# Local attention on one Trainium2 core: the fifth projection of a tile placed ahead of the second group's scores on TensorE

## What is computed

```python
def attn_layer(x, Wqkv, qs, ksc, Wo):          # x (8, 256, 128); 16 heads of 64
    q, k, v = jnp.split(x @ Wqkv, 3, -1)       # 3 x 1024 columns
    q, k = l2norm(q) * qs, l2norm(k) * ksc     # per head
    q = q * cos * scale + rotate_half(q) * sin * scale
    k = k * cos * inv + rotate_half(k) * sin * inv
    out = local_attention(q, k, v)             # windows of 32, each sees itself and the one before
    return out @ Wo

def ffn_layer(x, g, bln, W1, b1, W2, b2):
    a, gate = jnp.split((layernorm(x) * g + bln) @ W1 + b1, 2, -1)
    return a * gelu(gate) @ W2 + b2

for i in range(6):
    x = attn_layer(shift_tokens(x), ...) + x
    x = ffn_layer(shift_tokens(x), ...) + x
```

## Time and profile before

| what | value |
|---|---|
| median of 3 runs | 2246.68 us (2245.82 to 2247.02) |
| the profiled execution | 2248.77 us, its span 2247.0 us |
| TensorE matmul busy | 2105.5 us, 94% |
| TensorE weight load busy | 1439.5 us, 64% |
| VectorE busy | 1842.6 us, 82% |
| ScalarE busy | 1660.0 us, 74% |
| GpSimd busy | 1654.5 us, 74% |
| mean granted TensorE clock | 0.979 |

### The profile page before, as it was taken

How to read it: one execution, slowest core, us unless ns; L and a number is a source line. 1 busy time by engine, 2 the same in 40 slices (tenths; PEclk the granted TensorE clock), 3 DMA queues, 4 the chain that set the end, 5 groups by cost and what they waited for, 6 DMA issues and landing times. The chain is left out here.

```text
span 2247.0 us, 70768 instructions
## 1 busy us (share of the span) xinstructions
PE 2105.5 (94%) x26387; PEld 1439.5 (64%) x26387; DVE 1842.6 (82%) x2689; ACT 1660.0 (74%) x3300; POOL 1654.5 (74%) x1553
## 2 busy tenths in 40 slices
PE   5899869999889999999999999999999999999995
PEld 3555436666646676667676676667667666676764
DVE  4898967777778888888888888888888888888883
ACT  5898845454368788788878878887887887888773
POOL 4677852333378888888888888888888888888881
PEclk8999999999999999999999999999999999999996
DMA  2222220000012223232322322232232222223221
GB/s 77 104 69 67 64 77 1 2 1 1 8 47 77 70 61 79 71 81 61 81 70 59 81 70 76 67 79 72 59 81 70 71 72 74 78 58 82 70 66 45
DMA packets 103501, 140.43 MB, mean 62 GB/s; under 512 B 63376, under 2 KB 64400, under 8 KB 103056
## 3 DMA queue, kind: packets, MB, share of 16 engines
q1 hardware_dynamic: 103440, 139.64, 23.0%
HBM read 56.39 MB, written 1.31 MB: 26 GB/s over the span
## 5 line engine op out<-in xcount | busy, mean ns | idle before, releaser
L1740 PE MATMUL f_psA<-f_W,f_xT 128*128 (+1 forms) x1154 | 603.4, 619 | 7.7 <-ACT f_Vt L1492 3.6
L1630 DVE TENSOR_TENSOR f_m<-f_psA,f_tab 128x1024 f32<-128x1024 f32 x385 | 460.0, 1215 | 78.5 <-ACT f_sq L1474 78.5
L1410 POOL TENSOR_TENSOR f_qkr<-f_qkr,f_rn 128x1024 f32<-128x1024 f32 x192 | 361.4, 1904 | 17.2 <-POOL f_rn L1433 17.2
L1381 POOL TENSOR_TENSOR f_Pr<-f_Pr,f_rden 128x384 f32<-128x384 f32 x384 | 308.1, 835 | 87.2 <-DVE f_rden L1619 87.2
L1474 ACT ACTIVATE f_sq<-f_psA 128x512 f32<-128x512 f32 x385 | 222.2, 590 | 107.0 <-PE f_psA L1740 103.5
L1740 PEld LDWEIGHTS f_psA<-f_W,f_xT 128*128 128x128 f32 x1154 | 192.6, 190 | 131.2 <-issue 90.5
L1606 DVE TENSOR_REDUCE f_mx<-f_psS 128x8 f32<-128x768 f32 x192 | 183.9, 958 | 83.6 <-PE f_psS L1775 83.6
L1400 POOL TENSOR_TENSOR f_qkr<-f_m 128x512 f32<-128x512 f32 x192 | 244.7, 1274 | 7.5 <-DVE f_m L1630 7.5
L1401 POOL TENSOR_TENSOR f_qkr<-f_m 128x512 f32<-128x512 f32 x192 | 246.4, 1283 | 0.0
L795 POOL TENSOR_TENSOR x_Es<-x_E 128x512 f32<-128x512 f32 x64 | 81.4, 1272 | 188.8 <-PE x_psO L1012 127.7
L1661 DVE TENSOR_REDUCE f_ssq<-f_sq 128x32 f32<-128x2048 f32 x96 | 218.5, 2276 | 0.0
(11 more groups left out here) (176 smaller groups left out, 4710.8 us busy)
## 6 DMA issues: line engine op xcount, KB each, us to landing
f_V<-f_Vt SPq DMA_DIRECT2D x96, 384.0 KB, 4.5
f_V<-f_Vt SPq DMA_DIRECT2D x96, 256.0 KB, 3.7
f_W<-in_f_W SPq DMA_DIRECT2D x48, 344.0 KB, 4.6
m_Cb<-m_BC_rows SPq DMA_DIRECT2D x64, 256.0 KB, 3.2
f_W<-in_f_W SPq DMA_DIRECT2D x48, 296.5 KB, 4.2
f_V<-f_Vt SPq DMA_DIRECT2D x48, 128.0 KB, 2.3
f_xsA<-xall SPq DMA_DIRECT2D x98, 32.0 KB
f_xsA<-xall SPq DMA_DIRECT2D x98, 31.8 KB
```

What stands on the lines that cost most here:

```text
L1381: pool.tensor_tensor(pv, pv, rv.unsqueeze(3).broadcast_to([P, 2, 2, KEYS]), ALU.mult).then_inc(Pr_ready[g][j], 1)
L1410: pool.tensor_tensor(qv, qv, rv.unsqueeze(3).broadcast_to([P, 2, GH, DH]), ALU.mult).then_inc(qkr_ready[g], 1)
L1630: dve.tensor_tensor(m12[:, j, :, half].rearrange("p m (h d) -> p m h d", d=DH), psA[n % 2][:, :].rearrange("p (h d) -> p h d", d=DH).unsqu ...
L1740: pe.matmul(psA[n % 2][:, :], xT[:, t, :], weights(i, W_QKV + n * 512, 512), start=True, stop=True).then_inc(A_full[n_fill], 1)
```

## The change

Projection 4 moves from point 8 of the list to a place between points 5 and 6: behind `times_v(1)` and ahead of `scores(1)`. Its wait on `A_free[2]` goes with it. Nothing else is added, removed or moved; the other engines' programs are the same.

```diff
@@ -1882,6 +1882,9 @@
                 if "C" in stages:
                     times_v(0)
                     times_v(1)
+                if "A" in stages:
+                    pe.wait_ge(A_free[2], u + 1)
+                    project(u, i, t, 4)
                 if "B" in stages:
                     scores(1)
                 if "E" in stages:
@@ -1895,9 +1898,6 @@
                     for tt in range(TPB):
                         ins = pe.transpose(psD[0][:, tt * P:(tt + 1) * P], hatC[:, tt, :], ident[:, :])
                     ins.then_inc(xn_full, 1)
-                if "A" in stages:
-                    pe.wait_ge(A_free[2], u + 1)
-                    project(u, i, t, 4)
                 if "C" in stages:
 
                     weights_here(pe, i - 1, share_of(W_2))
```

## The result

The changed kernel takes 2267.38 us (median of 4 runs, 2266.81 to 2268.53) against 2246.25 us for the kernel before in the same session: a ratio of 1.0096, 95% interval 1.0079 to 1.0114. It is slower by 21 us; forecast were 18. The profiled execution has a span of 2266.7 us, 19.7 more than before, at the same mean clock of 0.979.

What follows compares the result with a forecast made beforehand. It took a loop through TensorE for most of a slot, and VectorE at `scores(1)`, to set the pace. D slot + 0.52 and E slot - 0.12 us, times 46 pairs, added 18.4 us: 2265.1 us, range 2248 to 2282.

Steps and rivals of the forecast that it cites:

- The delay of `scores(1)`: On TensorE, the second group's scores start 0.74 us later, behind a 0.17 us step and a 1.05 us projection.
- TensorE's own balance: On TensorE, 0.74 us lost at the scores, 0.86 won back behind: output projection and next slot 0.12 us earlier.
- End of the D slot: Through ScalarE, 0.22 us of the delay is absorbed; the Gelu and first square hold TensorE to + 0.52 us.
- End of the E slot: Through VectorE, the residual sum and the square of projection 0 come out level at the table product: -0.12 us.
- Sum: Whole loop: + 0.52 - 0.12 = + 0.40 us per pair, 46 pairs, + 18.4 us, median 2265.1 us.
- a plain tie: On TensorE at `w1(0, 2)`: it had just arrived there, at 1414.37, the product's start, when the Gelu ended.
- hardly anything else holds TensorE up for long: On TensorE, the 0.27 us wait ahead of `scores(1)`, 89 times, was read as nearly the only long one.
- the faster case: TensorE saves 0.42 us per slot and the delay, 0.44 us, is absorbed: 2237 us; chance 0.13.
- The cheap case: On TensorE, the projection costs 0.86 us in its new place too, delay 0.55 us: + 1 us, 2248; chance 0.10.
- That VectorE passes its delay too: In the E slot, VectorE is 0.19 us late at the table product: + 0.71 per pair, 2279 us; chance 0.12.
- The change between tiled and whole-array work: On TensorE, switching costs 0.15 to 0.23 us going in and 0.19 us in the projection.

Runs made afterwards that it cites:

- e1: The kernel before with the whole projection 4 ahead of the second group's scores in D slots only: 2271.39 us, ratio 1.0111.
- e3: The changed kernel with the second group's exponentials taken over 4 of 8 heads in D slots: 2253.17 us.
- e5: The changed kernel with the third Gelu behind the squares and its product behind the transposes of q and k: 2250.65 us, ratio to before 1.0014.
- e4: The kernel before with the second group's exponentials taken over 4 of 8 heads in D slots: 2238.15 us, ratio 0.9958.
- e6: The kernel before with the third Gelu behind the squares and its product behind the transposes of q and k: 2235.78 us, ratio 0.9952.
- e10: The kernel before with the first half of projection 4 early in both kinds of slot, the Gelu where it was: 2244.36 us, ratio 0.9987.
- e8: The kernel before with projection 4 early, whole in E slots and its first half in D slots, and the third Gelu behind the squares: 2228.52 us, ratio 0.9920.
- e9: The kernel before with the first half of projection 4 early in both kinds of slot and the third Gelu behind the squares: 2226.91 us, ratio 0.9909.

## Why the prediction was right

The forecast was 2265.1 us and + 18.4; measured 2267.4 and + 21. The sum was built per pair (33.25 us predicted, 33.26 measured), so each term can be laid beside the trace.

- *The delay of `scores(1)`*: 0.74 predicted, 0.72 measured. The projection's 1.05 us in its new place was 1.06, the step ahead of it 0.15 us and not 0.17. The price came from projection 1, which stood in the same surroundings; with the 0.86 us of the old place the forecast's own sum gives 2248.
- *TensorE's own balance*: 0.12 us won predicted, 0.15 measured at the start of the output projection. In the D slot the output projection then takes 0.05 us longer (1420.75 - 1418.91 = 1.84 us against 1.78), which the forecast did not have; it costs nothing here, because the Gelu holds TensorE anyway.
- *End of the D slot*: + 0.52 predicted. From the start of `times_v(1)` to projection 2 of the next slot it is 1425.19 - 1415.60 = 9.59 us against 1416.06 - 1406.98 = 9.08: + 0.51. e1 shows it alone (+ 0.52 us per pair, + 24.8 us), e3 and e5 show that it runs through ScalarE: shorten the chain by 0.32 us and 0.33 us per pair come back; take the Gelu out of the way of the squares, 0.37 us, and 0.36 us come back, where the same two edits give 0.19 and 0.23 us in the kernel before.
- *End of the E slot*: - 0.12 predicted. 1442.59 - 1432.30 = 10.29 us against 1433.55 - 1423.17 = 10.38: - 0.09. TensorE reaches the transposes of q and k 1441.30 - 1432.30 = 9.00 us behind `times_v(1)` and before 1432.31 - 1423.17 = 9.14, so it is 0.14 us early; 0.05 of this is lost to VectorE, with which the forecast had the squares level. The rows of these starts that were not shown yet, projection 2 of the changed kernel

```profile
1442.59 1.12 PE L1740 MATMUL f_psA<-f_W,f_xT 128*128 x2
```

and, before,

```profile
1423.17 1.10 PE L1815 MATMUL f_psP<-f_PT,f_V 96*64 96x64 f32 x32
```

- *Sum*: + 0.42 per pair, times 46 is 19.3 us, and the spans differ by 19.7. (Between D slots' `scores(1)` a pair is + 0.41.)

What was off lies in the reading of the kernel before. The text held that TensorE arrived at the E slot's gate product as the Gelu ended, and took this for a plain tie: nothing to be gained by a shorter chain on ScalarE. e4 (8.5 us) and e6 (11 us) show a cost in that tie, in the two projections behind it. The sentence that hardly anything else holds TensorE up for long was read from its matmul rows alone; the weight loads' waits for the Gelu and for VectorE, 27.3 and 20.4 us, stood in the same list. It did not hurt the forecast, since the chain only got longer; for a change that shortens the chain the same reading would have been wrong, as the expectations of e4 and e6 were.

The rivals: the faster case needed a projection of 0.86 us in the new place, and it took 1.06. The cheap case the same. That VectorE passes its delay too did not come about, but it was near: neither of its two idle times is left, and some 0.05 us per pair do reach TensorE. The change between tiled and whole-array work does have a price here, 0.15 us for the step and 0.2 us in the projection. The Trainium skill (TensorEngine Tiling (Array Packing), Tiling Modes, Key Properties) states that changing the tiling mode drains TensorE, without a figure. The trace agrees that there is a price; what part of it is a drain and what part the weights that could not be loaded ahead, no run here separates. The prediction counts two such changes more per slot, which takes the 96x64 and the 64x64 tiles for one mode; no run here tests that. This price decided that TensorE won 0.15 us and not 0.42. Paid on TensorE alone it did not make the kernel slower, since TensorE still won. But it is part of the delay: by the forecast's sum a delay of 0.55 us, without the 0.19 us in the projection, would have cost 1 us in all. The loss takes both, the price that makes `scores(1)` 0.72 us late and a chain on ScalarE that can take only 0.22 us of it.

## What to carry to other kernels

Work that is put into a wait of the busiest engine delays whatever came after the wait, and if that heads a chain through other engines, its slack there must be larger than the delay: read it at every link, in every kind of iteration, before the move. Here the whole projection lost in the D slot and gained in the E slot. Half of it gained in the E slot, still lost 0.08 us in the D slot where ScalarE had nothing more to give (e10), and gained in both only with the Gelu moved (e8, e9). A wait that ends just as the work arrives is not free either: look at the weight loads' rows, and not only at the matmuls'. The time that a piece costs is the time it takes between its new neighbours: 1.06 us between tiled products, 0.86 between whole-array ones.

## What the runs showed of the hardware

- A projection (two records, 512 columns, fp32) takes 0.86 us from start to start when its weights are in ahead and whole-array work follows, 0.95 us when tiled work follows (1409.28 to 1410.23 in e6), and 1.05 when it also comes behind tiled work or starts on a release. The late weights show as a recorded length of 1.12 us and not 1.02, with no idle time on the matmul row; the weight load then starts with the matmul (1417.18 for both, before) and not 0.11 us ahead (1409.47 and 1409.58).
- Halving the elements of an exponential on ScalarE (768 to 384 per partition) took it from 0.84 to 0.52 us: 0.2 us of it don't shrink.
- The load of the activation table took 1.28 us in every D slot (48 of 48), and the Gelu started right behind it (1421.63 + 1.28 to 1422.92).
- TensorE's matmul busy time rose with the same instructions. The first rows of the page after:

```profile
span 2266.7 us, 70768 instructions
...
PE 2130.0 (94%) x26387; PEld 1431.2 (63%) x26387; DVE 1836.6 (81%) x2689; ACT 1657.0 (73%) x3300; POOL 1654.9 (73%) x1553
```

That is 24.5 us more than 2105.5, at the same share of 94%. The share of busy time says nothing here of whether the span got longer.
